# Identity matmuls in front of TensorE's long waits, and another order of the delta rule's steps, in a fused macaron block on one core

## The chip, the cores and the metric

The kernel runs on one core of a Trainium2 chip. Time is device microseconds for one execution, as the median of several. PE is TensorE, DVE VectorE, ACT ScalarE, POOL GpSimd, and SP the engine that issues the DMAs. All arithmetic is f32.

## The reference, cut to what matters

x is 1024 rows of 256. Six layers follow each other, each on the layernorm of x and added to x:

```python
x = x + 0.5 * L0_ffn(ln(x))     # feed-forward 0: silu gate and up, 256 -> 704 -> 256
x = x + L0_attn(ln(x))          # 16 heads, rope, window of 64, difference of two softmaxes
x = x + 0.5 * L0_ffn(ln(x))     # feed-forward 1, the same weights
x = x + 0.5 * L1_ffn(ln(x))     # feed-forward 2: 688 wide, its weights are lut[idx]
x = x + L1_attn(ln(x))          # the delta rule, 16 heads of 128
x = x + 0.5 * L1_ffn(ln(x))     # feed-forward 3
```

The delta rule, for each of 16 heads, with q, k, v from a convolution of four taps and silu:

```python
def step(S, inp):
    qt, kt, vt, gt, bt = inp
    S = S * gt[..., None]
    pred = jnp.einsum('bhk,bhkv->bhv', kt, S)
    delta = (vt - pred) * bt[..., None]
    S = S + kt[..., None] * delta[:, :, None, :]
    o = jnp.einsum('bhk,bhkv->bhv', qt, S)
    return (S, o)
```

Then o is normed, multiplied by sigmoid of a second gate and projected back to 256.

## The kernel before, in words

Each engine has one instruction stream in a fixed order, and streams meet by semaphores. A feed-forward goes in two halves of 512 rows: `ln_turn` transposes the normed rows on PE with the identity (eight transposes), ACT copies them to XT, `ffn_up` forms gate and up tile by tile, DVE multiplies them, `ffn_down` forms the sum. While feed-forwards 0 and 1 run, ACT and DVE also look up the weights of the L1 feed-forward in the table (L1096 and L1484) and SP writes them out; feed-forwards 2 and 3 load them back (`w_scratch`), which `w_loaded` tells.

The delta rule treats a head in 8 chunks of 128 rows. For a head n the steps are: "piece" 0 to 7 (projections into banks 0 and 1), convolutions, "norm" (sums of squares), seven "level" steps that build the triangular products of a chunk, "advance" on DVE that folds in the decay, the inverse of 16x16 blocks on DVE ("invert", "less") with a round trip by DMA, then "left" and "right" products that double the inverse, "keys" (transposes), and the scan over the chunks: "predict" c (L992, L993), "solve" c (L1004), "update" c (L1011, L1012). The scan is a chain through all three engines: predict on PE, a difference on DVE (L1741), solve on PE, a copy on ACT (L1310), update on PE, the state on DVE (L1752) and the output's copy and square on ACT (L1319, L1320). Last come "final", "turn_out" and, for every second head, "project" 0 to 3, whose sums DVE adds to x (L1785).

The steps of up to three heads are interleaved. PLACE holds, for each engine, each step with a number; step s of head n goes at n plus that number, and the sorted list is the engine's stream. So the numbers are an order and no times, and the order may differ between engines. Banks: pieces, gate and norm take 0 or 1, level and left 2 or 3, right 4, the scan 5 and 6, keys, turn_out and project 7. `use` waits until the bank's reader is done.

Head 0 has no scan of an earlier head beside it, and head 15 no pieces of a later one; the heads between are called steady here. `dr_prelude` stands before head 0: eight transposes, the products of the two low-rank gates (L844), beta (L849), which SP stores before it loads the first heads' weights (`d_w`).

## Time and profile before

| what | value |
| --- | --- |
| median of 3 runs | 1650.01 us (1649.91 to 1652.41) |
| the profiled execution | 1646.93 us, its span 1645.1 us |
| mean granted TensorE clock | 0.939 of 2.4 GHz |
| busy: PE, DVE, ACT, POOL | 1426.6, 1202.7, 1013.0, 42.8 us |
| share of the span | 87%, 73%, 62%, 3% |
| PE instructions | 14936 |
| attention, about | 90 to 382 us |
| delta rule, about | 538 to 1564 us |

A busy PE is not PE at its peak, since ends are modelled and matmuls overlap: a step's cost is best read from start to start. The bracket at the end of a row of the timeline is the engine's idle time before it and who ended it.

### The profile page before, as it was taken

The numbers are of one execution on the slowest core, as the hardware profiler recorded it, in microseconds if no ns is written. First come the engines' busy times: TensorE is split into PE (matmuls) and PEld (weight loads), VectorE is DVE, ScalarE is ACT, GpSimd is POOL, SyncE is SP. The second block draws the span as 40 slices with busy tenths as digits, with TensorE's granted clock in tenths as the row PEclk, the third lists the DMA queues.
The fourth block names the chain that finished last, engine by engine and source line by source line (L and its number), as shares of the span: only waits on it lengthen the run. The fifth ranks groups of instructions, "written<-read, shape, count | busy, mean of one in ns | idle before, by whom it ended". The sixth has DMA issues, their size and how long they took to land. (4 is left out here: it accounts for less than half of the span.)

```text
span 1645.1 us, 41414 instructions
## 1 busy us (share of the span) xinstructions
PE 1426.6 (87%) x14936; PEld 943.0 (57%) x14936; DVE 1202.7 (73%) x3775; ACT 1013.0 (62%) x2716; POOL 42.8 (3%) x49
## 2 busy tenths in 40 slices
PE   6887889978889678999998999989989899878688
PEld 2544555654445235566666766766666667567434
DVE  6848888965832377889888888998988898883131
ACT  5517888985610456677777777786777777743120
POOL 0000000000000000000000000000000000000000
PEclk9989899988999876999999999999999999978599
DMA  4025000000020211112121212212121211100010
GB/s 165 14 68 126 15 21 21 3 1 0 1 80 0 79 30 31 36 53 61 25 62 53 46 42 61 59 23 59 57 62 19 67 55 30 42 26 13 0 54 26
DMA packets 128488, 69.28 MB, mean 42 GB/s; under 512 B 104464, under 2 KB 115984, under 8 KB 127264
## 3 DMA queue, kind: packets, MB, share of 16 engines
q1 hardware_dynamic: 128288, 66.64, 15.1%
q8 instruction: 123, 2.02, 0.5%
q14 instruction: 77, 0.63, 0.1%
HBM read 51.36 MB, written 6.98 MB: 35 GB/s over the span
## 5 line engine op out<-in xcount | busy, mean ns | idle before, releaser
L1631 DVE SCALAR_TENSOR_TENSOR arena<-arena 128x1024 f32<-128x1024 f32 x144 | 184.6, 1282 | 30.0 <-ACT arena L1200 28.9
L862 PE MATMUL bank<-xt,arena 128*128 128x512 f32 x384 | 191.2, 631 | 5.3 <-ACT arena L1192 3.9
L1709 DVE TENSOR_TENSOR arena<-arena 128x512 f32<-128x512 f32 x224 | 156.4, 698 | 18.7 <-PE bank L915 13.6
L709 PE MATMUL bank<-xt,arena 128*128 128x512 f32 x320 | 142.1, 600 | 3.8 <-DVE arena L1443 3.8
L862 PEld LDWEIGHTS bank<-xt,arena 128*128 128x128 f32 x384 | 71.0, 201 | 70.6 <-issue 69.2
L709 PEld LDWEIGHTS bank<-xt,arena 128*128 128x128 f32 x320 | 60.2, 192 | 86.2 <-issue 86.0
L1310 ACT COPY arena<-bank 128x128 f32<-128x128 f32 x128 | 33.8, 264 | 121.0 <-PE bank L1004 120.3
L728 PE MATMUL bank<-arena 128*128 128x256 f32 (+2 forms) x384 | 97.0, 399 | 6.2 <-DVE arena L1443 5.3
L1199 ACT COPY arena<-bank 128x512 f32<-128x512 f32 x96 | 56.8, 592 | 72.1 <-PE bank L862 67.1
L1131 ACT ACTIVATE arena<-arena 128x128 f32<-128x128 f32 x256 | 99.5, 393 | 0.0
L1711 DVE TENSOR_TENSOR arena<-arena 128x256 f32<-128x256 f32 x224 | 94.3, 421 | 0.0
L728 PEld LDWEIGHTS bank<-arena 128*128 128x128 f32 (+2 forms) x384 | 69.0, 192 | 35.2 <-issue 20.5
L915 PEld LDWEIGHTS bank<-arena 128*32 128x32 f32 x5120 | 58.6, 114 | 48.5 <-issue 34.0
L1011 PE MATMUL bank<-arena 128*128 128x128 f32 x256 | 61.9, 325 | 27.4 <-ACT arena L1310 26.3
L758 PE MATMUL bank<-xt,arena 128*128 128x512 f32 x160 | 79.1, 636 | 6.6 <-DVE arena L1535 5.6
L915 PE MATMUL bank<-arena 128*32 128x32 f32 x5120 | 72.0, 204 | 13.1 <-ACT arena L1211 4.6
L974 PEld LDWEIGHTS bank<-arena 64*64 64x64 f32 x2048 | 69.0, 141 | 23.8 <-DVE arena L1733 17.3
L1558 DVE CUSTOM_DVE_ANT_0 arena<-bank,arena 128x128 f32<-128x128 f32 x256 | 63.8, 287 | 21.9 <-issue 18.7
L974 PE MATMUL bank<-arena 64*64 64x32 f32 x2048 | 76.1, 226 | 2.2 <-DVE arena L1733 1.3
L1085 ACT ACTIVATE arena<-bank 128x512 f32<-128x512 f32 (+1 forms) x24 | 14.3, 596 | 101.6 <-PE bank L709 74.6
L1484 DVE SCALAR_TENSOR_TENSOR arena<-arena,small_vectors 128x1072 f32<-128x1072 f32 x60 | 76.7, 1328 | 0.0
L814 PE MATMUL bank<-arena 128*128 128x256 f32 x256 | 66.4, 398 | 5.0 <-DVE x L1602 5.0
(168 smaller groups left out, 3307.5 us busy)
## 6 DMA issues: line engine op xcount, KB each, us to landing
arena<-d_w SPq DMA_DIRECT2D x16, 519.0 KB, 6.7
arena<-beta_scratch SPq DMA_DIRECT2D x16, 512.0 KB, 5.3
arena<-zero_scratch SPq DMA_DIRECT2D x14, 512.0 KB, 4.3
arena<-arena SPq DMA_DIRECT2D x64, 64.0 KB, 2.5
arena<-zero_scratch SPq DMA_DIRECT2D x15, 256.0 KB, 3.0
arena<-arena SPq DMA_DIRECT2D x12, 256.0 KB, 3.8
arena<-w_scratch SPq DMA_DIRECT2D x2, 1376.0 KB, 6.1
arena<-f_idx SPq DMA_DIRECT2D x2, 1072.0 KB, 8.5
```

The costliest lines, as they stand in the source:

```text
L709: last = pe.matmul(bank[2 * w + n % 2][0:rows, :], (WU if f < 2 else WU1R)[:, w, k, m * P:m * P + rows], XT[:, k, hf * HALF:(hf + 1) * HAL ...
L728: last = pe.matmul(bank[4 + pair][:, j * D:(j + 1) * D], HT[0:rows, hf, m, t * P:(t + 1) * P], (WD if f < 2 else WD1)[0:rows, m, :], start ...
L758: last = pe.matmul(bank[6 + a][:], w, XT[:, k, hf * HALF:(hf + 1) * HALF], start=(k == 0), stop=(k == KC - 1))
L814: last = pe.matmul(bank[5][:, t % 2 * D:(t % 2 + 1) * D], OT[:, 4 * (g % 2) + h, t * P:(t + 1) * P], WO[:, 4 * g + h, :], start=(h == 0), ...
L862: last = pe.matmul(bank[b][:], DW[:, par, c:c + P], XT[:, k, rhs], start=(k == 0), stop=(k == KC - 1))
L915: last = pe.matmul(to.rearrange("p (w b s) -> p w b s", w=2, s=s), KL[:, par, r], rhs, start=True, stop=True)
L974: last = pe.matmul(to, left, moved, start=True, stop=True)
L1131: last = act.activation(EX[:, p % 2, i, a, :], SMK[:, p % 2, i, a, :], ACT.Exp, bias=NMX[:, p % 2, i, a:a + 1], scale=-1.0, accum_out=ES[: ...
L1484: last = dve.scalar_tensor_tensor(out=W1[:, cs], in0=AWAY[:, k % PENS, cs], scalar=value, in1=W1[:, cs], op0=ALU.subtract, op1=ALU.min)
L1631: dve.scalar_tensor_tensor(out=CT[:, x], in0=RAW[:, x, 3 - j:3 - j + S], scalar=DW[:, par, tap:tap + 1], in1=CT[:, x], op0=ALU.mult, op1=A ...
L1709: dve.tensor_tensor(kq, kq, left, ALU.mult)
L1711: dve.tensor_tensor(kl, kl, t[:, :, 1, :].broadcast_to([P, nb // 2, s]), ALU.mult).then_inc(kq_step, 1)
```

## The change

Two things. First, `keep(b, k)` puts k matmuls of the identity by itself into bank b, with no wait of their own. `keep` with 18 stands ahead of the transposes of the second and the last feed-forward and of the delta rule, and ahead of the third feed-forward's wait for its weights. `fill` does it ahead of the waits of the steps that FILL names: in head 0 and 1 before pieces 7, before level 0 of group 1, before piece 4 of head 1 and before left 4 of group 0 in head 0; in the last head one before each predict, solve and update from chunk 2 on, 12 and 3 before the output's turns and 3 before project 2. That makes 178 matmuls. Second, the numbers in PLACE are others, for PE, ACT and DVE.

```diff
+FILL = {(0, "piece", 7): 14, (1, "piece", 7): 14, (0, "level", 0, 1): 14, (1, "piece", 4): 8, (0, "left", 4, 0): 20,
+        (H - 1, "turn_out", 0): 12, (H - 1, "turn_out", 1): 3, (H - 1, "project", 2): 3}
+FILL.update({(H - 1, what, c): 1 for what in ("predict", "solve", "update") for c in range(2, NT)})
...
             def ffn(f, u):
+                if f == 2:
+                    keep(0, 18)
                 pe.wait_ge(w_loaded, W_COUNT[f])
...
+            def keep(b, k):
+
+                for _ in range(k):
+                    pe.matmul(bank[b][:, 0:P], ident[:], ident[:], start=True, stop=True)
+
+            def fill(n, *step):
+
+                keep(6 if n < 2 else 2, FILL.get((n, *step), 0))
...
             def dr_prelude():
+                keep(0, 18)
                 ln_turn(4, 1)
...
             def dr_piece(n, par, j):
 
+                fill(n, "piece", j)
...
             if count > 2:
+                keep(0, 18)
                 ln_turn(2, 0)
                 ffn(1, 2)
...
             if count > 5:
+                keep(2, 18)
                 ln_turn(5, 0)
                 ffn(3, 5)
```

`fill` stands in the same way at the head of `dr_level`, `dr_left`, `dr_predict`, `dr_solve`, `dr_update`, `dr_turn_out` and `dr_project`. Of the table, two lines:

```diff
 "pe": [
-        (2.966, "predict", 6), (2.979, "solve", 6), (3.021, "update", 6), (3.048, "predict", 7), (3.103, "solve", 7),
+        (2.979, "predict", 6), (3.007, "solve", 6), (3.048, "update", 6), (3.075, "predict", 7), (3.103, "solve", 7),
```

What stands in a row on PE in head 0, from the level 6 products to the first left and right products, before (L922 and L926 are levels, L871 gate, L878 norm, L945 left, L974 right):

```order
L922 MATMUL bank3<-arena 64x2x32 x8
L926 MATMUL bank2<-arena 64x128 x4
L871 MATMUL bank0<-arena 128x512
L871 MATMUL bank1<-arena 128x512
L926 MATMUL bank3<-arena 64x128 x4
L878 MATMUL bank0<-arena 128x512
L945 MATMUL bank2<-arena 64x64 x8
L945 MATMUL bank3<-arena 64x64 x8
L974 MATMUL bank4<-arena 64x32 x16
L878 MATMUL bank1<-arena 128x512
L974 MATMUL bank4<-arena 64x32 x16
```

and now (L941 and L945 with 128 columns are levels, L889 gate, L896 norm, L965 left, L994 right):

```order
L941 MATMUL bank3<-arena 64x2x32 x8
L945 MATMUL bank2<-arena 64x128 x4
L889 MATMUL bank0<-arena 128x512
L945 MATMUL bank3<-arena 64x128 x4
L889 MATMUL bank1<-arena 128x512
L896 MATMUL bank0<-arena 128x512
L896 MATMUL bank1<-arena 128x512
L843 MATMUL bank6<-ident 128x128 x20
L965 MATMUL bank2<-arena 64x64 x8
L965 MATMUL bank3<-arena 64x64 x8
L994 MATMUL bank4<-arena 64x32 x32
L965 MATMUL bank2<-arena 64x64 x8
```

The second norm went from between the right products to before the left ones, and twenty identity matmuls (L843) stand behind it.

PE in a steady head, around the scan's last two chunks, before (L992 and L993 predict, L1004 solve, L1011 and L1012 update):

```order
L1004 MATMUL bank5<-arena 128x128
L945 MATMUL bank2<-arena 64x64 x8
L945 MATMUL bank3<-arena 64x64 x8
L1011 MATMUL bank5<-arena 128x128
L1012 MATMUL bank6<-arena 128x128
L974 MATMUL bank4<-arena 64x32 x16
L992 MATMUL bank5<-arena 128x128
L993 MATMUL bank6<-arena 128x128
L878 MATMUL bank1<-arena 128x512
L974 MATMUL bank4<-arena 64x32 x16
L1004 MATMUL bank5<-arena 128x128
L945 MATMUL bank3<-arena 64x64 x8
```

and now (L1013 and L1014 predict, L1027 solve, L1035 and L1036 update):

```order
L896 MATMUL bank1<-arena 128x512
L1027 MATMUL bank5<-arena 128x128
L965 MATMUL bank2<-arena 64x64 x8
L965 MATMUL bank3<-arena 64x64 x8
L1035 MATMUL bank5<-arena 128x128
L1036 MATMUL bank6<-arena 128x128
L994 MATMUL bank4<-arena 64x32 x16
L1013 MATMUL bank5<-arena 128x128
L1014 MATMUL bank6<-arena 128x128
L1027 MATMUL bank5<-arena 128x128
L994 MATMUL bank4<-arena 64x32 x16
L965 MATMUL bank2<-arena 64x64 x8
```

The norm in bank 1 (L896) stands ahead of solve 6, and solve 7 comes straight behind predict 7, ahead of the right product.

DVE in a steady head, around the first sum of a projection, before (L1741 predict's difference, L1652 a decay's product, L1709 and L1711 advance, L1785 the sum, L1752 the state, L1631 convolution):

```order
L1741 TENSOR_TENSOR arena<-arena,bank5 128x128
L1652 TENSOR_TENSOR arena<-arena 128x32
L1709 TENSOR_TENSOR arena<-arena 128x2x8x32
L1711 TENSOR_TENSOR arena<-arena 128x8x32
L1785 TENSOR_TENSOR x<-bank7,x 128x512
L1752 SCALAR_TENSOR_TENSOR arena<-arena,bank5 128x128
L1631 SCALAR_TENSOR_TENSOR arena<-arena 128x1024
```

and now (L1770, L1681, L1738 and L1740, L1814, L1781, L1660):

```order
L1770 TENSOR_TENSOR arena<-arena,bank5 128x128
L1681 TENSOR_TENSOR arena<-arena 128x32
L1738 TENSOR_TENSOR arena<-arena 128x2x8x32
L1740 TENSOR_TENSOR arena<-arena 128x8x32
L1660 SCALAR_TENSOR_TENSOR arena<-arena 128x1024
L1681 TENSOR_TENSOR arena<-arena 128x16
L1814 TENSOR_TENSOR x<-bank7,x 128x512
L1781 SCALAR_TENSOR_TENSOR arena<-arena,bank5 128x128
L1660 SCALAR_TENSOR_TENSOR arena<-arena 128x1024
```

The sum (L1814) stands behind a convolution step and a decay's product.

## Rows read from the trace of the kernel before

**Rows 1.** Busy us of each engine by stretch, granted clock (PEclk), DMA.

```profile
core 0: us, PE busy (x) PEld busy (x) DVE busy (x) ACT busy (x) POOL busy (x), PEclk, DMA share, GB/s
558.50:566.10 7.60, 6.23 (x11) 2.42 (x11) 0.01 (x1) 3.62 (x6) 0.00 (x0) 0.78 0.66 197
586.80:600.50 13.70, 8.51 (x145) 4.42 (x148) 11.84 (x24) 8.00 (x10) 0.00 (x0) 0.53 0.25 79
633.80:657.80 24.00, 22.72 (x336) 18.78 (x337) 13.81 (x35) 13.36 (x22) 0.00 (x0) 0.50 0.09 29
1514.20:1543.50 29.30, 22.71 (x75) 17.06 (x76) 5.14 (x15) 5.86 (x29) 0.00 (x0) 0.50 0.00 1
764.90:1448.60 683.70, 628.57 (x9135) 451.36 (x9138) 606.18 (x1681) 506.98 (x1177) 20.99 (x13) 0.99 0.19 49
```

**Rows 2.** The timeline of PE, second feed-forward: start, us, line, shapes, [idle <-releaser].

```profile
387.08 1.97 PE L684 MATMUL bank<-ident,arena 128*128 128x128 f32 x8 [5.22 <-DVE arena L1425]
389.77 3.68 PE L701 MATMUL bank<-xt,arena 128*64 128x512 f32 x8 [0.72 <-issue]
...
411.40 1.04 PE L684 MATMUL bank<-ident,arena 128*128 128x128 f32 x8
413.16 1.94 PE L701 MATMUL bank<-xt,arena 128*64 128x512 f32 x8 [0.73 <-ACT xt L1074]
415.03 3.70 PE L709 MATMUL bank<-xt,arena 128*128 128x512 f32 x8
```

**Rows 3.** The timeline of PE at the third feed-forward.

```profile
467.02 3.39 PE L701 MATMUL bank<-xt,arena 128*48 128x512 f32 x8 [3.62 <-DMA arena<-w_scratch]
```

**Rows 4.** The timeline of PE, and of its weight loads, at the delta rule's start.

```profile
538.63 1.97 PE L684 MATMUL bank<-ident,arena 128*128 128x128 f32 x8 [5.21 <-DVE arena L1425]
541.37 8.96 PE L844 MATMUL bank<-xt,arena 128*128 128x512 f32 x16 [0.77 <-ACT xt L1074]
...
558.51 1.81 PE L864 MATMUL bank<-arena 128*128 128x512 f32 x2 [4.65 <-DMA arena<-d_w]
...
541.34 0.50 PEld L844 LDWEIGHTS bank<-xt,arena 128*128 128x128 f32 x2 [1.14 <-DMA arena<-sel_in]
```

**Rows 5.** The timeline of PE, and of DVE, in head 0.

```profile
593.11 1.08 PE L915 MATMUL bank<-arena 128*32 128x32 f32 x64 [4.29 <-DVE arena L1672]
...
633.88 1.97 PE L945 MATMUL bank<-arena 64*64 64x64 f32 x32 [3.88 <-DMA arena<-inverse_turned_scratch]
...
600.97 0.73 DVE L1709 TENSOR_TENSOR arena<-arena 128x512 f32<-128x512 f32 x1 [1.73 <-PE bank L915]
```

**Rows 6.** The timeline of PE in the last head's scan, one chunk.

```profile
1526.63 0.80 PE L992 MATMUL bank<-arena 128*128 128x128 f32 x2 [0.62 <-ACT arena L1320]
...
1527.86 0.77 PE L1004 MATMUL bank<-arena 128*128 128x128 f32 x2
1529.03 0.77 PE L1011 MATMUL bank<-arena 128*128 128x128 f32 x2 [0.40 <-ACT arena L1310]
1529.59 0.64 PE L1012 MATMUL bank<-arena 128*128 128x128 f32 x2
1530.85 0.80 PE L992 MATMUL bank<-arena 128*128 128x128 f32 x2 [0.62 <-ACT arena L1320]
```

**Rows 7.** The timeline of PE in a steady head, the same steps.

```profile
1034.29 0.38 PE L992 MATMUL bank<-arena 128*128 128x128 f32 x2
1034.51 0.39 PE L993 MATMUL bank<-arena 128*128 128x128 f32 x2
1035.10 0.46 PE L1004 MATMUL bank<-arena 128*128 128x128 f32 x2 [0.20 <-DVE arena L1741]
...
1036.57 0.49 PE L1011 MATMUL bank<-arena 128*128 128x128 f32 x2
1036.89 0.39 PE L1012 MATMUL bank<-arena 128*128 128x128 f32 x2
```

**Rows 8.** The timeline of PE behind the last scan.

```profile
1548.18 1.12 PE L1024 MATMUL bank<-ident,arena 128*128 128x128 f32 x4 [4.10 <-ACT arena L1333]
```

**Rows 9.** The view of waits of DVE in two steady heads: total, times, longest.

```profile
DVE x L1785 <- PE bank L1038: 2.1, 2, 1.2
```

More of the change, by code:

```diff
@@ new lines @@
+        (2.034, "left", 4, 1), (2.062, "right", 4, 0), (2.116, "right", 4, 1), (2.13, "left", 5, 0), (2.144, "left", 5, 1),
+        (2.185, "right", 5, 0), (2.212, "keys", 0), (2.24, "right", 5, 1), (2.253, "left", 6, 0), (2.295, "right", 6, 0),
+        (2.308, "left", 6, 1), (2.336, "keys", 1), (2.349, "solve", 0), (2.377, "right", 6, 1), (2.404, "update", 0),
+        (2.473, "predict", 1), (2.527, "solve", 1), (2.568, "update", 1), (2.61, "predict", 2), (2.623, "solve", 2),
+        (2.651, "update", 2), (2.719, "predict", 3), (2.747, "solve", 3), (2.76, "update", 3), (2.788, "predict", 4),
@@ L87 @@
[L87 to L89 removed]
+        (0.412, "piece", 7), (0.465, "piece", 2), (0.482, "piece", 3), (0.518, "piece", 1), (0.553, "piece", 0),
+        (0.623, "silu", 1), (0.675, "piece", 6), (0.693, "exp_z"), (0.763, "square", 1), (0.781, "piece", 4),
@@ new lines @@
+        (0.816, "piece", 5), (0.868, "ln_z"), (1.061, "norm", 0), (1.079, "norm", 1), (1.096, "exp_k"), (1.132, "exp_g"),
+        (1.202, "silu", 2), (1.237, "silu", 0), (1.289, "square", 0), (1.36, "turn_v", 1), (1.605, "level", 5, 0),
+        (1.64, "turn_v", 0), (1.728, "flip"), (1.851, "level", 5, 1), (1.904, "gate", 0), (1.921, "level", 6, 0),
+        (1.956, "level", 6, 1), (1.974, "gate", 1), (2.009, "left", 4, 0), (2.026, "left", 4, 1), (2.149, "left", 5, 1),
+        (2.167, "left", 5, 0), (2.254, "keys", 0), (2.272, "left", 6, 0), (2.307, "right", 6, 0), (2.325, "left", 6, 1),
@@ L114 @@
+        (4.18, "project", 3),
     ],
```

76 lines of the change are left out of this document (35 added, 41 removed).

## The prediction

> **What bounds the kernel now.** I read the page's slices first, then the view of stretches, the timeline of PE at each place where its clock is low, and last the waits. The page has PE at 87% of the span, DVE at 73% and ACT at 62%, and a granted clock below full in the slices around the feed-forwards, in head 0 of the delta rule and at its end. The mean of 0.939 over 1645.1 us, with levels of 2.4 and 1.2 GHz, makes (1 - 0.939) x 2 x 1645.1 = 200 us at 1.2 GHz. The reader is to see two regimes. In the twelve heads from 764.9 to 1448.6 the clock is 0.99, PE is busy 628.6 of 683.7 us and DVE 606.2 (92% and 89%): both are near full, neither is idle long, and what sets the head's 57.0 us is how the two in-order streams mesh [rows 1]. Everywhere else a low clock follows an idle PE: behind 5.22 us of idle a run of eight turns takes 1.97 us where 24 us later it takes 1.04 [rows 2]; behind 3.62 us the gate of the third feed-forward takes 3.39 [rows 3]; in the last head's scan PE waits 0.62 and 0.40 us in each chunk, and the whole of 29.3 us has the clock at 0.50 [rows 1, 6].
>
> **What an added matmul costs.** One identity matmul is 128x128x128 in f32 and shows as two PE instructions, like the scan's products. Such a pair moves the next one by 0.22 us at full clock (L992 to L993) and at most by 0.32 (L1011 to L1012) [rows 7]; at 1.2 GHz by 0.56 at most (L1011 to L1012) [rows 6], and by twice 0.22 where nothing else holds it. I take 0.22 and 0.43, since the fillers have no operand to wait for. Eighteen are 4.0 us, fourteen 3.1, twenty 4.4. They stand ahead of PE's waits, so they cost nothing while they end before what PE waits for, and the excess in full if they don't. They write banks that nobody reads then; no other engine waits for them.
>
> **The feed-forwards.** Before the second one PE idles 5.22 us; 4.0 us of filler fit. If the clock stays, the turns to the gate take 411.40 to 413.16 = 1.76 us in place of 387.08 to 389.77 = 2.69, the gate 1.94 in place of 3.68, and the first products behind it some 0.8 less: 3.5 us [rows 2]. Behind it DVE's table look-ups run nearly without a gap until the weights are written out, and they start with the first gate, so I carry 3.3 (bounds 0 and 3.6). Before the third, 4.0 us of filler stand in 3.62 us: +0.4, against 3.39 -> 1.94 and 0.1 behind: -1.1 (bounds +0.4 and -1.5) [rows 2, 3]. The last one has 18 as well, but its weights land after the turns, so PE idles again behind them: I take -0.7, between nothing and the -1.5 of its like.
>
> **The delta rule's start.** 5.21 us of idle take 18. The turns gain nothing, for the weight load behind them already waited 1.14 us for the masks' DMA; of sixteen 128x512 matmuls in 8.96 us, eight would take 3.5 to 3.7 at full clock, so 7.0 to 7.4: -2.0 (bounds 0 and -3) [rows 2, 4]. Then SP stores beta and loads the head's weights, so this term moves the 558.51 with it. Fourteen (3.1 us) fit in the 4.65 us there [rows 4]. The next 7.6 us have a clock of 0.78, all PE work that ACT follows: 7.6 x 0.22 = -1.7 (bounds 0 and -1.7) [rows 1].
>
> **Head 0.** From 586.8 to 600.5 the clock is 0.53, but DVE is busy 11.8 of 13.7 us, so most of PE's lateness is covered. What shows is DVE's 1.73 us behind a slow piece [rows 1, 5]; the two runs of fourteen fit (4.29 us of idle before the second): -1.5 (bounds 0 and -3). The eight before piece 4 of head 1 stand under DVE's and SP's inverse, which PE's first left product waits for at 633.88: nothing. The twenty before that product need 4.4 us where 3.88 are free: +0.5 [rows 5]; norm 1, which now stands in that gap too, leaves its old place among the right products, which is even. The 24 us behind it are wholly at 1.2 GHz with PE busy 22.7: if all of it went at 2.4 GHz, up to 11 would come back [rows 1]. But in the steady heads, at 0.99, these small products stand between wide ones, and here they stand nearly alone, with DVE's steps between them. I take a quarter, -2.5, so -2.0 with the excess (bounds +0.5 and -9).
>
> **The tail.** One chunk takes 1526.63 to 1530.85 = 4.22 us at 1.2 GHz [rows 6]. At full clock, step by step: predict to solve 0.81 in place of 1.23; solve to update 1.17 less 0.31 (0.77 against 0.46 for the pair) = 0.86; the update's two products 0.32 + 0.39 in place of 0.56 + 0.64; then 0.62 of ACT as before: 3.00 us [rows 6, 7]. The fillers (one before each predict, solve and update from chunk 2) take 0.22 in gaps of 0.62, 0.20 and 0.40, so they fit at full clock. At 1.2 GHz they take 0.43 each, and the one before solve has no gap: +0.43 a chunk. Filled, such a chunk has eight pairs of 0.43 in some 4.65 us, 74% of PE against 51% now. I take it that this lifts the clock after one chunk: 0.4 - 5 x 1.22 = -5.7. Behind the scan twelve (2.6 us) stand in 4.10 us [rows 8]; the eight output turns then save 1.0 as the eight turns do above, and the first projection, at half of 3.70 us when full and twice that when not, 1.6 [rows 2]. Together -8.3.
>
> **The order table.** No work is added or taken: the same steps, as many table loads on ACT. In a steady head norm 1 now stands between predict 6 and solve 6 on PE, solve 7 comes straight behind predict 7, and ACT empties gate 1's bank earlier to allow it. On DVE the projections' sums stand behind a convolution step and a product, which covers the 2.1 us that DVE now waits for them in two heads [rows 9]: at best 7 x 2.1 = -15. Against that, PE meets new waits at norm 1 and solve 7. I take -2 for the fourteen heads.
>
> **Sum.** 3.3 + 1.1 + 0.7 + 2.0 + 1.7 + 1.5 + 2.0 + 8.3 + 2 = 22.6 us. The profiled execution took 1646.9 us (span 1645.1), so 1624.3; the median of the runs shown is 3.1 above it, so 1627.
>
> **Rivals.** (B) The scan's clock stays at 1.2 GHz. For it: single matmuls between waits leave PE idle in every chunk, and chunks at 51% never lifted the clock in 29.3 us [rows 1, 6]. Against it: 74%. Then the scan costs 6 x 0.43 = +2.6, the twelve take 5.2 us in 4.10 (+1.1), and about -2.6 comes back behind them: +1 in place of -8.3, so 1637. The Trainium skill bears on this one ("TensorE: Matmul & The Clock Gate", section "A second HAM failure mode: psum-queue depth-cycling"): a matmul stream with short idle spells between its groups can swing between the two levels, because each spell costs a re-throttle. By that rule the scan keeps falling back and this rival's time holds; no row of before shows a filled scan.
>
> (C) The order costs time in steady heads, and the kernel is slower. Place: solve 7 on PE, straight behind predict 7, with right 4 1 and both left 5 queued behind it. DVE must first finish right 4 0 and then predict 7's difference. Before, norm 1 and right 4 1 (a microsecond each) ran in that time; now PE stands for up to 1.1 us, and the inverse's products, which DVE waits for, come as much later, so up to 2.2 us a head: 14 x 2.2 = 31, less 20.6, gives 1660. It decides from 20.6 / 14 = 1.5 us a head. For it: PE has only 8% to give [rows 1]. Against it: the scan ends earlier by the same move.
>
> (D) The order gains what DVE waits now: -15 in place of -2, so 1614 [rows 9]. Against it: DVE's wait may only move to the next step.
>
> (E) The fills do nothing because the low clock comes from narrow products and not from the idle time: the 24 us with PE busy 22.7 speak for that in head 0 alone [rows 1]; the turns of rows 2, wide and slow, speak against it. It is in the range as part of B.
>
> **How the numbers follow.** Forecast 0.50, its own range 1618 to 1637; B 0.18 (with E); D 0.18; C 0.14. About 0.2%, 3.3 us, can be told from no change. Faster: 0.50 + 0.17 + 0.18, and 0.02 of C where the order costs under 1.2 us a head: 0.87. Within 0.2%: 0.03 of C and 0.01 of B: 0.04. Slower: 0.09. The range goes from halfway into D, 1610, to 1648, which holds B whole and the cheaper part of C.
>
> **What would show it.** Right: the turns before the second feed-forward in 1.1 us and its gate in 1.9; the loads of d_w some 6 us earlier; a clock near 1.0 from the third chunk of the last scan, 3.0 us a chunk; twelve steady heads in 684 us or a little less. Wrong in a step: 1.97 us turns behind a filled gap; chunks of 4.6 us; left 4 0 starting after its DMA and the products behind it at 1.2 GHz throughout. The forecast falls if PE's new waits at norm 1 and solve 7 are over 1.5 us a head and the head is longer by as much.

## The result and the profile after

| kernel | median, us | runs | ratio to before (95%) |
| --- | --- | --- | --- |
| before | 1650.83 | 1649.91 to 1652.41 (4) | |
| changed | 1630.77 | 1626.38 to 1637.29 (4) | 0.9881 [0.9843, 0.9918] |

The change makes the kernel 1.2% faster, 20 us; 1627 was forecast, with 1618 to 1637 as the likeliest case's own range. The profiled execution of the changed kernel is the slowest of its four: 1637.29 us, its span 1635.5, with a mean granted clock of 0.954. So the two traces differ by only 9.6 us. Times of the chip's slower state are left out everywhere: one execution of the kernel before (1669.41 us) and one without the scan's fillers (1735.87 us, clock 0.82).

Line numbers move by 5 to 29: L684 is now L689, L701 L706, L844 L861, L864 L882, L945 L965, L974 L994, L992/L993 L1013/L1014, L1004 L1027, L1011/L1012 L1035/L1036, L1018 L1042, L1024 L1050, L1038 L1065, L1741 L1770, L1785 L1814. The filler is L843.

The timeline of PE at the second and third feed-forwards, which answers to [rows 2, 3] (start, us, line, shapes, [idle <-releaser]):

```profile
382.44 4.18 PE L843 MATMUL bank<-ident 128*128 128x128 f32 x36
387.82 1.09 PE L689 MATMUL bank<-ident,arena 128*128 128x128 f32 x8 [1.20 <-DVE arena L1454]
389.69 1.94 PE L706 MATMUL bank<-xt,arena 128*64 128x512 f32 x8 [0.77 <-issue]
...
460.73 4.29 PE L843 MATMUL bank<-ident 128*128 128x128 f32 x36
464.94 1.93 PE L706 MATMUL bank<-xt,arena 128*48 128x512 f32 x8
```

The 5.22 us of idle are now 4.18 of filler and 1.20 of idle, and behind them the turns take 1.09 in place of 1.97 and the gate 1.94 in place of 3.68. At the third feed-forward nothing is idle ahead of the gate, which takes 1.93 in place of 3.39.

The delta rule's start and head 0, for [rows 4, 5]:

```profile
535.09 1.09 PE L689 MATMUL bank<-ident,arena 128*128 128x128 f32 x8 [0.99 <-DVE arena L1454]
537.51 7.13 PE L861 MATMUL bank<-xt,arena 128*128 128x512 f32 x16 [1.32 <-DMA arena<-sel_in]
...
553.76 1.13 PE L882 MATMUL bank<-arena 128*128 128x512 f32 x2 [1.45 <-DMA arena<-d_w]
...
583.07 4.91 PE L843 MATMUL bank<-ident 128*128 128x128 f32 x28
587.92 0.81 PE L934 MATMUL bank<-arena 128*32 128x32 f32 x64
...
622.85 4.63 PE L843 MATMUL bank<-ident 128*128 128x128 f32 x40
627.41 1.15 PE L965 MATMUL bank<-arena 64*64 64x64 f32 x32
...
635.46 1.92 PE L994 MATMUL bank<-arena 64*64 64x32 f32 x32 [0.80 <-issue]
```

The sixteen 128x512 matmuls take 7.13 us in place of 8.96. Two fillings leave nothing idle behind them: the one ahead of level 0, part of which ran at 1.2 GHz (4.91 us where its twin took 3.29), and the twenty ahead of the first left product. The left products start at 2.4 GHz and later fall to 1.2 (1.92 us for the last row; it is 1.12 at full clock).

The last head's scan, for [rows 6], and behind it, for [rows 8]:

```profile
1516.82 0.80 PE L1013 MATMUL bank<-arena 128*128 128x128 f32 x2 [0.20 <-ACT arena L1349]
...
1520.57 0.49 PE L1013 MATMUL bank<-arena 128*128 128x128 f32 x2
...
1523.65 0.49 PE L1013 MATMUL bank<-arena 128*128 128x128 f32 x2 [0.40 <-ACT arena L1349]
1523.98 0.39 PE L1014 MATMUL bank<-arena 128*128 128x128 f32 x2
1524.20 0.39 PE L843 MATMUL bank<-ident 128*128 128x128 f32 x2
1524.57 0.46 PE L1027 MATMUL bank<-arena 128*128 128x128 f32 x2
1524.87 0.39 PE L843 MATMUL bank<-ident 128*128 128x128 f32 x2
1525.43 0.46 PE L1035 MATMUL bank<-arena 128*128 128x128 f32 x2 [0.18 <-ACT arena L1339]
...
1536.31 2.94 PE L843 MATMUL bank<-ident 128*128 128x128 f32 x24
1540.48 0.66 PE L1050 MATMUL bank<-ident,arena 128*128 128x128 f32 x4 [1.22 <-ACT arena L1362]
...
1543.86 1.97 PE L1065 MATMUL bank<-arena 128*128 128x256 f32 x8 [1.04 <-DVE arena L1801]
```

A chunk from 1520.57 takes 3.08 us in place of 4.22. The clock rises between the first filled predict and the second.

The view of stretches (us, busy us of PE, PEld, DVE, ACT and POOL, then granted clock, DMA share and GB/s). The first is the twelve heads of [rows 1], then the head behind them, then the stretch up to head 15's statistics:

```profile
754.46:1445.14 690.68, 638.99 (x9110) 462.20 (x9110) 601.06 (x1681) 511.97 (x1176) 19.59 (x13) 0.97 0.19 48
1445.14:1503.01 57.87, 50.11 (x724) 42.22 (x723) 35.61 (x126) 20.75 (x66) 1.63 (x2) 0.81 0.13 27
1503.01:1537.48 34.47, 27.89 (x192) 23.04 (x189) 7.43 (x24) 11.29 (x49) 1.63 (x2) 0.80 0.00 1
```

The twelve heads are 7 us longer than before. PE is busy 639.0 us in place of 628.6 with the same work, and the clock is 0.97 in place of 0.99. So what made them longer in this execution is largely slower matmuls. A place where it happens, the timeline of PE:

```profile
854.96 1.15 PE L965 MATMUL bank<-arena 64*64 64x64 f32 x32 [0.80 <-issue]
...
859.58 0.46 PE L1027 MATMUL bank<-arena 128*128 128x128 f32 x2 [1.14 <-DVE arena L1770]
859.97 1.92 PE L994 MATMUL bank<-arena 64*64 64x32 f32 x32
861.70 1.95 PE L965 MATMUL bank<-arena 64*64 64x64 f32 x32
```

Solve 7 (L1027, at 859.58) waits 1.14 us for DVE's difference among narrow products, and from there PE is at 1.2 GHz until about 870.

### The profile page after: what moved, and what is told of

The parts are those of the page before. It is cut to its first block and busy times, and to the rows that moved or that the text cites. A ratio compares the mean times of both kernels' runs of the same rounds, so it can differ in the third digit from the quotient of the medians.

```text
span 1635.5 us, 42126 instructions
## 1 busy us (share of the span) xinstructions
PE 1454.1 (89%) x15292; PEld 982.3 (60%) x15292; DVE 1195.9 (73%) x3775; ACT 1019.2 (62%) x2716; POOL 41.2 (3%) x49
## 5 line engine op out<-in xcount | busy, mean ns | idle before, releaser
L1660 DVE SCALAR_TENSOR_TENSOR arena<-arena 128x1024 f32<-128x1024 f32 x144 | 182.9, 1280 | 27.1 <-ACT arena L1229 26.8
L1738 DVE TENSOR_TENSOR arena<-arena 128x512 f32<-128x512 f32 x224 | 155.8, 695 | 7.6 <-PE bank L934 2.7
L1740 DVE TENSOR_TENSOR arena<-arena 128x256 f32<-128x256 f32 x224 | 94.6, 422 | 0.0
L994 PEld LDWEIGHTS bank<-arena 64*64 64x64 f32 x2048 | 69.7, 143 | 26.6 <-DVE arena L1762 12.7
L994 PE MATMUL bank<-arena 64*64 64x32 f32 x2048 | 76.7, 228 | 5.2 <-DVE arena L1762 3.3
L1587 DVE CUSTOM_DVE_ANT_0 arena<-bank,arena 128x128 f32<-128x128 f32 x256 | 63.8, 287 | 22.1 <-issue 18.7
L1339 ACT COPY arena<-bank 128x128 f32<-128x128 f32 x128 | 33.7, 263 | 73.9 <-PE bank L1027 73.7
L1035 PE MATMUL bank<-arena 128*128 128x128 f32 x256 | 63.1, 330 | 15.1 <-ACT arena L1339 15.1
L1027 PEld LDWEIGHTS bank<-arena 128*128 128x128 f32 x256 | 43.6, 195 | 45.9 <-DVE arena L1770 32.3
```

What stands on the lines that cost most here:

```text
L994: last = pe.matmul(to, left, moved, start=True, stop=True)
L1587: last = dve.tensor_tensor_reduce(SMK[:, p % 2, i, a, :], bank[2 * (p % 2) + i][:, a * P:(a + 1) * P], MASK[:, 0 if p % NT == 0 else 1, :] ...
L1660: dve.scalar_tensor_tensor(out=CT[:, x], in0=RAW[:, x, 3 - j:3 - j + S], scalar=DW[:, par, tap:tap + 1], in1=CT[:, x], op0=ALU.mult, op1=A ...
L1738: dve.tensor_tensor(kq, kq, left, ALU.mult)
L1740: dve.tensor_tensor(kl, kl, t[:, :, 1, :].broadcast_to([P, nb // 2, s]), ALU.mult).then_inc(kq_step, 1)
```

## How the profiles are compared

Each head has one POOL operation (its statistics, L1402), which cuts each trace at the same places; "mark n" is that of head n. In the changed kernel the first of these marks, for heads 0 and 1, are:

```profile
695.90 1.63 POOL L1402 TENSOR_TENSOR arena<-arena,minus_half 128x8 f32<-128x8 f32 x1 [162.28 <-DVE arena L1791]
754.46 1.63 POOL L1402 TENSOR_TENSOR arena<-arena,minus_half 128x8 f32<-128x8 f32 x1 [56.92 <-DVE arena L1791]
```

The table has for each profiled execution, in us: from the turns (the transposes) at the delta rule's start to head 0's first left product; from there to mark 0; the twelve heads from mark 1 to 13 and their granted clock; mark 13 to 14; 14 to 15; and from there to the end. Kernels are named as the experiments below; the last four rows are "more fillers" with six in place of twenty ahead of the left product, and that kernel with fillers in steady heads, in head 14, or in both.

| kernel | turns to left | left to 0 | 1 to 13, clock | 13 to 14 | 14 to 15 | to the end |
| --- | --- | --- | --- | --- | --- | --- |
| before | 95.3 | 74.7 | 683.7, 0.99 | 58.0 | 38.7 | 99.9 |
| changed | 92.3 | 68.5 | 690.7, 0.97 | 57.9 | 34.5 | 98.0 |
| changed, again | 93.1 | 67.9 | 684.5, 0.98 | 57.9 | 35.6 | 98.9 |
| fillers only | 92.2 | 66.3 | 692.9, 0.98 | 58.0 | 34.3 | 98.0 |
| order only | 97.9 | 68.8 | 685.9, 0.98 | 58.3 | 39.3 | 100.4 |
| the eighteens | 92.7 | 69.2 | 682.5, 0.99 | 58.0 | 37.0 | 102.0 |
| no twenty | 89.9 | 68.7 | 682.3, 0.99 | 57.9 | 32.1 | 97.9 |
| more fillers | 89.1 | 67.3 | 687.5, 0.98 | 58.2 | 31.1 | 96.3 |
| doubled | 101.7 | 71.0 | 681.5, 0.99 | 58.1 | 34.4 | 98.2 |
| more, with six | 88.7 | 69.8 | 687.8, 0.98 | 57.9 | 32.6 | 96.5 |
| six, and steady | 91.1 | 70.7 | 700.4, 0.98 | 56.9 | 31.8 | 96.4 |
| six, and head 14 | 91.3 | 69.9 | 682.8, 0.99 | 53.5 | 31.1 | 96.4 |
| six, and both | 88.7 | 70.2 | 701.9, 0.98 | 53.9 | 31.8 | 96.4 |

The column on the twelve heads shows where much of the spread between executions comes from. With the new order and no fillers in steady heads, so with one schedule in these twelve heads, there are nine profiles of eight kernels: four with a clock of 0.99 take 681.5 to 682.8 us, four with 0.98 take 684.5 to 687.8, and the one with 0.97 takes 690.7. Counted from the granted clock in stretches of 2 us, they have 10 to 35 us at 1.2 GHz, and the shortest have the least. The two profiles of the changed kernel itself are 6.2 us apart (690.7 and 684.5). So differences of under 9 us in this column say nothing of a kernel, and the experiments are judged by ratios over several rounds and, for one place, by that place's own rows. The kernel before ran beside each group; its medians there were 1656.91, 1654.97 and 1653.45, so only ratios are compared across groups. That kernel spreads as much as the changed one once it is run that often (1645.57 to 1663.74 us in 19 executions beside the first group), so the spread is no property of the change. The last columns have a spread too: the kernel without the twenty has the same code behind mark 14 as the changed one and takes 32.1 us to mark 15 where that takes 34.5 and 35.6.

## Experiments

### The parts alone: fillers, order, and the fillers of the scan

My theory after the first trace was that the new order, not the fillers, makes the steady heads slower.

Fillers only, with the order table of before (the diff is from the changed kernel, and shows one line of the table, cut short):

```diff
 PLACE = {
-        (0.226, "piece", 7), (0.432, "piece", 2), (0.486, "piece", 3), ...
+        (0.199, "piece", 7), (0.418, "piece", 2), (0.459, "piece", 3), ...
```

> All 178 identity matmuls, with the old order table. Theory A (the fills bring the gain, the new order costs time in the steady heads, because TensorE meets new waits there and its clock falls more often: fourteen heads took 807 us after, 798 before): about 1624, 6 to 9 us below the changed kernel and 24 to 28 below before. Theory B (the steady heads differ only by chance from run to run, the order is neutral): within 3 us of the changed kernel, about 1631. Theory C (the order is worth something at the ends, where head 0 and head 15 stand alone): 2 to 5 us above the changed kernel.

Measured 1635.93 us (1632.18 to 1637.92), ratio 0.9886 [0.9855, 0.9917]: within 1.5 us of the changed kernel beside it, as theory B had it.

Order only: the new table without any filler (again from the changed kernel, cut).

```diff
-FILL = {(0, "piece", 7): 14, ...
-                keep(0, 18)
...
```

> The new order table without any identity matmul. Theory A: 5 to 10 us above before, about 1657, with more stretches at 1.2 GHz in the steady heads than the two of before. Theory B: within 3 us of before, 1651. Theory C: 2 to 5 us below before.

Measured 1647.99 us (1641.22 to 1655.14), ratio 0.9959 [0.9934, 0.9983]: some 7 us below the kernel before, more than theory C had, and the opposite of A.

Fillers without the eighteen of the scan, old order:

```diff
-FILL.update({(H - 1, what, c): 1 for what in ("predict", "solve", "update") for c in range(2, NT)})
```

> The old order table with the fills but without the eighteen single ones of the last head's scan. If these single matmuls lift the clock in the scan (a chunk took 3.08 us after, 4.22 before): 6 x 1.1 = 6 to 7 us above the kernel with all fills and the old order. Rival (the twelve matmuls behind the scan and the scan's own work give the clock back anyway): within 2 us of it.

Measured 1640.46 us (1634.28 to 1646.32), ratio 0.9914 [0.9884, 0.9944]: 4.5 us above the kernel with all fillers and the old order, between the rival's 2 and the theory's 6 to 7. Its profile is not read.

The changed kernel again, beside these three:

> The changed kernel once more, beside the others on one chip: 1626 to 1637 with a spread of some 10 us between its runs, if the places where its clock falls in the steady heads change from run to run; a spread of 2 to 3 us, as before has, if the first 1637 was an outlier.

Measured 1634.45 us (1629.72 to 1642.80), ratio 0.9887 [0.9848, 0.9927]; its profiled execution had a span of 1630.6 us. The executions are 13 us apart, so the first 1637 was no outlier.

The theory fell. The order alone makes the kernel 0.4% faster, not slower, and the fillers with the old order have as long a row of steady heads as the changed kernel has (692.9 us). At an equal clock of 0.99 the new order's heads take 681.5 to 682.8 against 683.7, and with 21 us at 1.2 GHz in either trace 685.9 (order only) against 692.9 (fillers only). What the long steady heads of the first trace showed was the clock in that execution. The fillers are worth 1.1% by themselves, the scan's eighteen some 0.3% of it (4.5 us; the two intervals overlap). Order and fillers together give no more than the fillers alone, 0.9887 against 0.9886, where the sum of the parts would be 0.9845; with intervals of 0.4% on each side this is not proof that they overlap, but the table has a place where they do. From the first left product to head 0's mark the kernel before takes 74.7 us; the order alone brings it to 68.8, the fillers alone to 66.3, and both to 68.5 and 67.9. Each takes out of this stretch what the other would have. Part of what the order takes out it only moves: its left product starts 2.6 us later behind the turns, with norm 1 ahead of it (and one of SP's loads of the inverse took 1.76 us to issue in place of 0.43). From the turns to the mark it is 170.0 us before, 166.7 with the order alone, 158.5 with the fillers alone, and 160.8 and 161.0 with both. So in head 0 the fillers alone are the better version, by 2.3 us in these traces. In the old order norm 1 of head 1 stands among the right products, in the new one ahead of the left product, and in the trace of the order alone they are at 1.2 GHz for some 14 us in place of 24.

### The eighteens alone

```diff
-FILL = {(0, "piece", 7): 14, (1, "piece", 7): 14, ...
-FILL.update({(H - 1, what, c): 1 for what in ("predict", "solve", "update") for c in range(2, NT)})
+FILL = {}
```

The four runs of eighteen stay.

> The changed kernel with the new order, but with only the four runs of eighteen fillers (ahead of the turns of feed-forwards 1, 2 and 3 and of the delta rule's prelude); nothing is filled in the delta rule itself. Theory (each filled gap pays by itself, and the gains add up): the front, up to head 0's norm statistics, ends near 704.6 - 3.5 - 2 = 699 us, between the 704.6 of the order alone and the 695.8 of all fills; the last scan and what follows stay as without fills (39 and 100 us, less 1.5 for the last feed-forward); the ratio to the kernel before is 0.9959 - 5 to 7 us = 0.992 to 0.993. Rival (the gain of the fills is one thing: once the clock is up it stays up): the front ends within 1 us of 695.8. Rival (the fills of head 0 do it all): the front stays above 703.

Measured 1638.67 us (1635.68 to 1649.96), ratio 0.9916 [0.9881, 0.9952]. The front ended at 697.0, nearer to the rival's 695.8 than to the 699 of the theory. From the turns to the mark it takes 161.9 us, with all fillers 160.8 and 161.0: the seventy among the steps of heads 0 and 1 together bring about 1 us. That is a sum of two: by the next run fifty of them bring some 3 us (158.6) and the other twenty cost most of it. The tail has no fillers but the last eighteen and is 4.4 to 6.4 us longer than in the changed kernel (37.0 + 102.0 against 34.5 + 98.0 and 35.6 + 98.9).

### Without the twenty

```diff
-        (0, "left", 4, 0): 20,
```

> The changed kernel without the twenty fillers ahead of head 0's first left product. Theory (an idle PE lets the clock fall, fillers hold it): the left product starts some 0.5 us sooner, since nothing stands after norm 1 but the wait of about 4 us, and then the left and right products run at 1.2 GHz for 10 to 20 us; front mark 697.5 to 700 in place of 695.8, ratio 0.2% worse. Rival (narrow products keep the clock low whatever stands ahead): half the clock for as long as now, about 7 to 10 us, and a front mark of 695.3 to 696.

Measured 1628.51 us (1621.27 to 1636.33), ratio 0.9830 [0.9779, 0.9881]. The timeline of PE there:

```profile
622.41 1.98 PE L896 MATMUL bank<-arena 128*128 128x512 f32 x4
625.79 1.15 PE L965 MATMUL bank<-arena 64*64 64x64 f32 x32 [1.40 <-issue]
...
633.83 1.92 PE L994 MATMUL bank<-arena 64*64 64x32 f32 x32 [0.80 <-issue]
```

The left product starts 89.9 us after the delta rule's turns in place of 92.3 and 93.1, and from there to the mark it takes 68.7 in place of 68.5 and 67.9. Some 1.1 us of the first difference stand ahead of the first piece already, where the weights' load landed earlier in this execution (17.6 us behind the turns, against 18.7 and 18.8). The changed kernel's own trace tells the cost without that. SP issues the last load of the inverse at 624.74. Where PE waits idle for it, the left product starts 1.3 to 1.4 us behind this issue (624.49 and 625.79 without the twenty). With the twenty it starts at 627.41, so they held it up by some 1.3 us, and in the second profile (623.76 and 627.89) by 2.8. So here the fillers cost an estimated 1.3 to 2.8 us and brought under 1. The theory fell: the front mark came at 694.5, earlier than even the rival had it (695.3 to 696), and the clock stayed up no shorter than with the twenty. Whether narrow products are the reason for its fall is for the next run. The whole-kernel interval is too wide to show 2 us, the place's own rows are what the verdict rests on.

### More fillers

```diff
+        (0, "piece", 1): 5, (0, "piece", 6): 5, (0, "piece", 4): 9, (0, "level", 5, 1): 8,
+        (0, "right", 4, 1): 4, (0, "left", 5, 1): 4, (0, "right", 5, 0): 3,
+        (H - 1, "predict", 1): 6, (H - 1, "solve", 1): 1, (H - 1, "update", 1): 1,
-        (H - 1, "turn_out", 0): 12, (H - 1, "turn_out", 1): 3, (H - 1, "project", 2): 3}
+        (H - 1, "turn_out", 0): 12, (H - 1, "turn_out", 1): 3}
...
+                if f == 3:
+                    keep(0, 9)
...
             def dr_right(n, par, lv, gr):
+                fill(n, "right", lv, gr)
```

The three fillers ahead of project 2 are taken out with it.

> The changed kernel with fillers in the gaps that are still unfilled: 5, 5 and 9 ahead of head 0's pieces 1, 6 and 4, 8 ahead of its level 5 1, 4, 4 and 3 ahead of right 4 1, left 5 1 and right 5 0, 9 behind the first turns of the last feed-forward, and in the last scan 6 ahead of predict 1 and one each ahead of solve 1 and update 1. Theory: half-clock stretches 569-573, 613-621 and 634-642 go (PE is up to 3, 3 and 3 us sooner, of which DVE, ACT and the inverse's DMA cover about half), front 691 to 694 us; the last scan rises a chunk or two sooner, tail 32.5 to 33.5 us in place of 34.5 to 35.6; the last feed-forward 1 us: together 4 to 6 us, ratio 0.984 to 0.986. Rival (covered): the front mark moves by under 1 us, the total by under 2. Rival (excess): the fillers at 1.2 GHz end after the waits that they stand in, and the front is 1 to 2 us later.

Measured 1625.96 us (1616.51 to 1631.62), ratio 0.9808 [0.9767, 0.9850]: 0.7 to 0.8% below the changed kernel's two ratios, more than the theory's 4 to 6 us, with intervals that just touch. Head 0's left and right products, and head 15, in the view of stretches:

```profile
621.00:641.00 20.00, 19.46 (x419) 17.00 (x418) 14.51 (x37) 14.56 (x23) 0.00 (x0) 1.00 0.11 30
...
1494.41:1525.49 31.08, 25.05 (x208) 20.77 (x205) 7.44 (x24) 11.32 (x49) 1.63 (x1) 1.00 0.01 1
```

Both are at 2.4 GHz throughout. From the turns to head 0's mark it is 156.4 us against 160.8 in the changed kernel, and head 15 takes 31.1 against 34.5 and 35.6. Little of head 15's gain can be credited to them, since it took 32.1 in the last run without them. The gaps of 1.06, 1.18 and 0.80 us stood unfilled without the twenty as with them, which is why these had no say. At the last feed-forward nine more paid as well:

```profile
1547.63 1.09 PE L692 MATMUL bank<-ident,arena 128*128 128x128 f32 x8 [1.24 <-DVE arena L1460]
1548.56 2.17 PE L848 MATMUL bank<-ident 128*128 128x128 f32 x18
1551.24 1.92 PE L709 MATMUL bank<-xt,arena 128*48 128x512 f32 x8 [0.51 <-DMA arena<-w_scratch]
1553.10 17.43 PE L717 MATMUL bank<-xt,arena 128*128 128x512 f32 x40
```

The weights land at the same distance behind the turns (3.61 us; 3.75 in the changed kernel), and the gate then takes 1.92 us where the changed kernel's took 3.45: 5.47 us from turns to products against 7.13. With all these gaps filled, the same narrow products run at 2.4 GHz: they do not hold the clock down by themselves. The fillers are 128 columns wide, so these rows don't tell whether the work between them had to be wide or only had to be there.

### Doubled fillers ahead of the last head

```diff
-                keep(0, 18)
+                keep(0, 36)
-FILL = {(0, "piece", 7): 14, (1, "piece", 7): 14, (0, "level", 0, 1): 14, (1, "piece", 4): 8, (0, "left", 4, 0): 20,
+FILL = {(0, "piece", 7): 28, (1, "piece", 7): 28, (0, "level", 0, 1): 28, (1, "piece", 4): 16, (0, "left", 4, 0): 40,
```

> The changed kernel with twice as many fillers in each place ahead of the last feed-forward (36, 28, 16 and 40 in place of 18, 14, 8 and 20); the last head is as it was. It measures what a filler costs once its gap is full. With 0.11 us an instruction at 2.4 GHz: feed-forward 1, 4.0 more in 1.2 free; feed-forward 2, 4.0 more with nothing free; prelude, 4.0 in 1.0; piece 7 of head 0, 3.1 in 1.4; piece 7 of head 1, 3.1 in 2.2; level 0, 3.1 in 1.4; piece 4, 1.8 in up to 2.0; left, 4.4 with nothing free. Excess 2.8 + 4.0 + 3.0 + 1.7 + 0.9 + 1.7 + 0 + 4.4 = 18.5 us. Theory (the excess counts in full): front near 714 us, ratio near 1.000. Rival (slack behind the gap takes part of it): 703 to 709, ratio 0.993 to 0.997.

Measured 1647.08 us (1641.52 to 1650.77), ratio 0.9948 [0.9920, 0.9975]. The ratio is the rival's, the front the theory's: it ended at 715.9, 20.1 us behind the 695.8 of the changed kernel's second profile; the theory had 714 (18.5 us of excess). One run, doubled:

```profile
535.05 8.30 PE L843 MATMUL bank<-ident 128*128 128x128 f32 x72
543.19 1.04 PE L689 MATMUL bank<-ident,arena 128*128 128x128 f32 x8
```

Excess counts in full, at 8.30 / 36 = 0.23 us a filler. The ratio shows only part of it: the kernel is 0.6% slower than the changed one, not 1.2%. In its profile the steady heads are at their best (681.5), so the span is only 13.3 us above that of the changed kernel's second profile (1643.9 against 1630.6).

### Six in place of twenty, and the two groups on top

Six in place of twenty ahead of head 0's left product, on the kernel with more fillers:

```diff
-        (0, "left", 4, 0): 20,
+        (0, "left", 4, 0): 6,
```

> The kernel with more fillers, with 6 in place of 20 ahead of head 0's first left product. The runs without the twenty had the left product at 625.8 and with them at 627.9, and in the kernel with more fillers the twenty ended at 623.7 with nothing idle behind them. Theory: the wait there is over some 2 us earlier, six fill it, and the front mark falls from 691.0 to 689 to 690, ratio 0.1% better. Rival (the twenty were what kept the clock): half-clock stretch after the left products, front 692 or more.

Measured 1623.60 us (1617.24 to 1627.57), ratio 0.9816 [0.9795, 0.9837]. Here the theory failed, and the rival's front mark came true (693.9):

```profile
619.74 1.50 PE L848 MATMUL bank<-ident 128*128 128x128 f32 x12
624.07 1.51 PE L970 MATMUL bank<-arena 64*64 64x64 f32 x32 [2.83 <-issue]
625.32 1.92 PE L1000 MATMUL bank<-arena 64*64 64x32 f32 x32
```

The other fillers let PE arrive earlier, but the left product starts only 0.4 us earlier than behind the twenty (88.7 us against 89.1): 2.83 us are idle, and the clock falls with them, for 10 us, although the fillers between the narrow products are the same. In this kernel and the three below, which have the same six, the left product starts no earlier than 88.7 us behind the turns, and from it to the mark it takes 69.8 to 70.7 us in place of 67.3. From turns to mark it is 158.4 us with six against 156.4 with twenty. The same twenty that cost 1.3 us or more in the changed kernel were worth 2 in this one, because the gap was wide enough. The whole-kernel ratios (0.9816 and 0.9808) are too wide for this.

Steady heads, on top of that (the last three lines of the table put the like into heads 14 and 15):

```diff
+for n in range(1, H - 1):
+    LATE[(n, "left", 5, 1)] = (0, 1, n + 1, "norm", 0)
+    LATE[(n, "right", 5, 1)] = (0, 4, n + 1, "norm", 0)
+for n in range(H - 2):
+    LATE[(n, "solve", 7)] = (0, 3, n + 2, "norm", 0)
+LATE[(H - 2, "solve", 7)] = (0, 3, H - 1, "gate", 0)
+LATE[(H - 1, "left", 5, 1)] = (0, 1, H - 1, "gate", 0)
+LATE[(H - 1, "right", 5, 1)] = (0, 4, H - 1, "gate", 0)
...
+                if (n, *step) in LATE:
+                    b, k, *last = LATE[(n, *step)]
+                    pe.wait_ge(free[b], read(b, *last))
+                    keep(b, k)
```

> As the last, and in every steady head fillers in the three gaps that stand ahead of the places where the clock falls: 3 ahead of solve 7, 1 ahead of left 5 1, 4 ahead of right 5 1, into bank 0. Theory (idle PE among narrow products lets the clock fall in steady heads too): half-clock stretches between the first and the fourteenth mark go from 10 to 40 us to under 5, these twelve heads take 680 to 683 us in place of 682 to 691, the ratio is 0.2 to 0.4% better and the runs lie closer together. Rival (narrow products alone do it, or the place is chance): the same number of stretches as without, and the heads 0 to 0.3 us longer each from fillers that don't fit: ratio same or up to 0.2% worse.

Measured 1636.93 us (1631.53 to 1640.39), ratio 0.9896 [0.9877, 0.9915]: 0.8% slower than without. The timeline of PE in a steady head; L1046 is solve 7, L1032 predict 7, L857 the filler:

```profile
1092.41 0.49 PE L1032 MATMUL bank<-arena 128*128 128x128 f32 x2
...
1094.06 0.94 PE L857 MATMUL bank<-ident 128*128 128x128 f32 x6 [0.93 <-ACT arena L1290]
1094.83 0.39 PE L1046 MATMUL bank<-arena 128*128 128x128 f32 x2
...
1101.31 1.05 PE L857 MATMUL bank<-ident 128*128 128x128 f32 x8
1102.30 0.95 PE L1013 MATMUL bank<-arena 64*64 64x32 f32 x26
```

and the same steps without these fillers (the kernel with six):

```profile
1089.05 0.49 PE L1019 MATMUL bank<-arena 128*128 128x128 f32 x2
...
1090.54 0.46 PE L1033 MATMUL bank<-arena 128*128 128x128 f32 x2 [0.78 <-DVE arena L1776]
...
1097.63 0.95 PE L1000 MATMUL bank<-arena 64*64 64x32 f32 x26 [0.23 <-DVE arena L1768]
```

In steady heads every bank is in use. The filler needs one that is free, so it waits until ACT has read norm 0's (L1290); from predict 7 to solve 7 it is 2.42 us in place of 1.49. The gap ahead of right 5 1 is 0.23 us there, not the 1.10 of head 14 by which I had sized the four. The twelve heads take 700.4 us against 687.8, 1.05 a head. One schedule spreads by 9 us here, but the kernel with both groups takes 701.9 as well, and no profile without these fillers and with the new order is over 690.7. The price is over both theories. The clock fell as often as before, seven times against six in the twelve heads (by stretches of 2 us), so whether idle time or chance makes it fall in steady heads stays open; what is shown is the price.

Head 14, with the stretch where head 15 has no pieces of a later head beside it:

```diff
+LATE[(H - 2, "right", 5, 1)] = (1, 4, H - 1, "norm", 1)
+for step, k in ((("level", 2, 1), 1), (("level", 2, 0), 2), (("level", 3, 1), 3), (("level", 3, 0), 1)):
+    LATE[(H - 1, *step)] = (1, k, H - 1, "norm", 1)
+LATE[(H - 2, "predict", 2)] = (1, 4, H - 1, "norm", 1)
+LATE[(H - 2, "predict", 3)] = (0, 1, H - 1, "norm_q")
+LATE[(H - 2, "predict", 4)] = (0, 6, H - 1, "norm_q")
+LATE[(H - 2, "solve", 4)] = (0, 2, H - 1, "norm_q")
```

> As the first of this group, with 24 fillers in the gaps of the stretch where head 15 has no pieces of a later head beside it (ahead of right 5 1, levels 2 and 3, predict 2, 3 and 4 and solve 4). There five profiles in a row had 24 to 27 us at 1.2 GHz. Theory: the stretch keeps 2.4 GHz; of 25 us at half clock with PE busy throughout, 12 us of PE work come back, half of it covered by DVE: 5 to 7 us, ratio 0.3 to 0.4% better, the step between marks 13 and 15 from 112 to 106. Rival (DVE and the inverse's transfer bound this stretch, PE's lateness is covered): under 1.5 us.

Measured 1616.65 us (1611.22 to 1619.64), ratio 0.9766 [0.9749, 0.9783]. From mark 12 to 14, without them (first) and with them:

```profile
1382.12:1495.47 113.35, 100.09 (x1469) 77.92 (x1468) 84.36 (x265) 63.12 (x164) 3.27 (x2) 0.88 0.14 32
```

```profile
1382.81:1490.40 107.59, 96.80 (x1518) 76.34 (x1516) 84.45 (x265) 62.94 (x164) 3.27 (x3) 0.98 0.15 34
```

The kernel is 0.5% below the one with six, and the intervals don't touch. The clock rises from 0.88 to 0.98, PE is busy 3.3 us less although it does 49 instructions more, and 5.8 us are gone. Of these, 4.4 lie between marks 13 and 14 (57.9 to 53.5), and the kernel with both groups shows them too (53.9), where ten profiles without these fillers take 57.9 to 58.3. The other 1.4 lie in head 13, where only the four fillers ahead of right 5 1 stand, just before its end, and are within its spread. So the gain is a little under the 5 to 7 of the theory, and the rival's 1.5 is ruled out. Here pieces are missing, banks 0 and 1 are free, and the gaps are real.

All together:

```diff
 LATE = {}
+for n in range(1, H - 1): ...
+LATE[(H - 2, "right", 5, 1)] = (1, 4, H - 1, "norm", 1)
...
```

> All fillers of this group together. Theory: the gains add, total near 1610 us where the kernel before takes 1650, ratio 0.974 to 0.977, granted clock 0.98 or more. Rival (what bounds is no longer PE's clock): ratio within 0.1% of the best of the other three.

Measured 1637.49 us (1633.13 to 1647.15), ratio 0.9908 [0.9885, 0.9930]. The gains don't add, and both theories fail: its steady heads take 701.9 us, as in the kernel with steady fillers alone, and head 14's gain (53.9) stays. It has the highest granted clock of all, 0.973, and is 1.3% slower than the fastest. That one, fillers everywhere but in steady heads, is the version to keep: 2.3% below the kernel before, 1.2% below the changed one. By the rows above, twenty in place of six would likely bring some 2 us more (an estimate); no run shows it.

## Why the prediction was right, and where not

By the first profiled execution; "forecast" is the prediction's term. The rows add up to -10.4 where the spans differ by -9.6; most of the rest is the 0.7 us by which the second feed-forward starts later.

| step, from where to where | before | changed | moved | forecast |
| --- | --- | --- | --- | --- |
| second and third feed-forward (turns to turns) | 151.6 | 147.3 | -4.3 | -4.4 |
| the delta rule's start (turns to first piece) | 19.9 | 18.7 | -1.2 | -2.0 |
| first pieces and levels (to the first left product) | 75.4 | 73.7 | -1.7 | -2.7 |
| left products to head 0's mark | 74.7 | 68.5 | -6.2 | -2.5 |
| fourteen heads | 797.9 | 807.1 | +9.2 | -2 |
| head 15 up to predict 1 | 7.7 | 9.6 | +1.9 | 0 |
| its scan (predict 1 to final) | 29.3 | 23.4 | -5.9 | -5.7 |
| output turns | 9.0 | 7.9 | -1.1 | -1.0 |
| first projection | 4.3 | 2.8 | -1.5 | -1.6 |
| last feed-forward (turns to the products behind the gate) | 6.7 | 7.1 | +0.4 | -0.7 |

- **Feed-forwards.** Right: the idle time was the cause, and the length of the filling was free but for 0.4 us of the third.
- **The last feed-forward.** Wrong in sign. Its gate waits 2.65 us for the weights, as the prediction said it would; I still credited a part of the gain, and in that wait the clock falls again. The gate before and after:

```profile
1573.23 3.24 PE L701 MATMUL bank<-xt,arena 128*48 128x512 f32 x8 [1.57 <-DMA arena<-w_scratch]
1563.36 3.45 PE L706 MATMUL bank<-xt,arena 128*48 128x512 f32 x8 [2.65 <-DMA arena<-w_scratch]
```

What the faster turns gained, the gate waited longer. The gain is there for those who fill the gap behind the turns too: 1.7 us with nine more.

- **Delta rule's start and head 0's levels.** Right in sign, and 1.8 us too large over both rows. For the levels the term itself holds: without the twenty they come 3.1 us earlier (72.3 us), where -3.2 was forecast, and what the first trace lacks is the excess of the twenty. The start depends on when the weights' load lands, and shows -1.1 to -2.4 in the nine profiles with eighteen fillers there and the new order (17.5 to 18.8 us).
- **Left products.** More gain than forecast, and the cause I priced is only one of two. The fillers alone take 8.4 us out of this stretch, so a quarter of the 11 was too little. The order alone takes out 5.9, of which 2.6 come back ahead of the left product; I had put the move of norm 1 down as even. Together they bring no more than one of them. The excess of the twenty, put at 0.5 us, was mis-sized: it is 1.3 to 2.8, because norm 1's microsecond stands in the gap as well and PE is left with less to wait (1.40 us idle without the twenty, 3.88 before). Rival E, narrow products as the cause, falls with the run of more fillers, though what that run put between them was wide.
- **The scan.** Right to 0.2 us, by two small misses that offset each other: a chunk of 3.08 us against 3.00, and the first filled chunk took 3.75 us where 4.65 was taken, since the clock rose within it (1516.82 to 1520.57). The fillers' fit is as worked out, 0.62, 0.20 and 0.40 of gap against 0.22. Left out was head 15's opening: it lost 1.9 us in this execution because the clock fell there, ahead of the first filler; without the twenty, with the same code there, it fell only later, in the scan (32.1 us for the whole of head 15). Rival B is refuted by these rows: with fillings the scan holds 2.4 GHz through gaps of 0.40 and 0.18 us. The Trainium skill's account on which it drew ("TensorE: Matmul & The Clock Gate", section "A second HAM failure mode: psum-queue depth-cycling"), that frequent short idle spells between groups of matmuls cost a re-throttle, does not carry over to the filled scan; head 14's unfilled gaps, with a clock of 0.75 to 0.81, agree with it.
- **Steady heads.** The term was -2 and the profiled execution shows +9.2, and yet the runs don't show a step of the order's reasoning to fail. Over twelve runs the order alone is 0.4% faster. Solve 7 does wait (0.78 us, 1.14 once), as rival C had it, but at a clock of 0.99 the twelve heads are 0.9 to 2.2 us shorter, not 18 or more longer, and 7 us shorter in the two traces with 21 us at 1.2 GHz. How much the order brings in steady heads is not settled by that. DVE's waits for the projections' sums (12.7 us in the twelve heads before) are gone and others took their place, such as 15.2 us for the right products' bank, so rival D's objection was right as far as one trace tells. What the prediction lacked is that a steady head's clock isn't given: it took 0.99 from one execution for a constant, and in thirteen profiles it is 0.97 to 0.99, worth up to 9 us in one schedule.

So the forecast was near, in part by its working and in part by luck. By its working: outside the fourteen heads it has -20.6, and the two profiles of the changed kernel show -18.8 and -16.9, since the fillings' terms were sized by rows at both clock levels and the misses nearly cancel (left products on one side, the excess, head 15's opening and the last feed-forward on the other). By luck: the sum was made for the profiled execution, and those two profiles moved by 9.6 and 14.5 us, not 22.6; that the medians are 20 apart also hangs on where the clock fell in the steady heads of the executions compared.

## What to carry to other kernels

Fill an idle gap of TensorE only where the trace shows that the work behind it is both slow and waited for; count the filler at its time at either clock level, since excess is paid in full, and count again whatever the change itself moves into the gap. Fill the short gaps within a run of narrow products as well, and refit all of them after each step, since an earlier PE makes the later gaps wider. Where every bank is in use, a filler brings a wait with it, and a higher granted clock can go with a slower kernel; judge by spans of the same stretch, and take the clock of a stretch from several executions before charging a difference to the code.

## What the runs showed that I had not expected

- The same twenty fillers cost an estimated 1.3 to 2.8 us in one kernel and bring 2 in another, where the gap has 1.4 us without them in the one and 4.3 in the other (1.50 of the six and 2.83 of idle).
- Products of 64 columns and fewer hold 2.4 GHz once the gaps between them are filled with wider ones (clock 1.00 with PE busy 19.46 of 20.00 us).
- Between marks 13 and 14 the clock was 0.75 to 0.81 in all ten profiles without fillings there, with the old order and the new: where the next head has no pieces, the fall is no matter of chance, as it is in steady heads.
- The twelve steady heads of one and the same schedule differ by 9 us over nine executions (681.5 to 690.7 us), and by 6 in the one kernel that was profiled twice, with how often the clock falls.
